# One reduction over a pair of banks for each row maximum, two score banks, and a new grouping of the exponential sums in layer 1

## What is computed

```python
h = ada_norm(x, cond)                                   # layer 0: LayerNorm, scale and shift; layer 1: LN and modulation
q, k, v = h @ wq, h @ wk, h @ wv                        # 16 heads of 32; layer 0 with rotary; layer 1 with 4 key heads
a = softmax(q @ k.T / sqrt(32))                         # over 1024 keys
x = x + (a @ v) @ wo                                    # gated in layer 1
x = x + gelu(norm(x) @ w1 + b1) @ w2 + b2               # 512 -> 2048 -> 512, gated in layer 1
```

## Time and profile before

| | |
|---|---|
| median of the runs shown | 4044.38 us (4036.17 to 4044.77, 3 runs) |
| the profiled execution: time, span | 4039.97 us, 4038.1 us |
| TensorE's mean granted clock in it | 0.975 |
| attention of sequence 6 (layer 1): its blocks 0 to 6, its last block | about 3138 to 3346 us, 3346 to 3382 us of the span |
| attention of sequence 0 (layer 0) | about 129 to 435 us |
| start, before the first attention | 0 to 129 us |

### The profile page before, as it was taken

One profiled execution on the slowest core, in us unless ns is written; L12 is line 12 of the kernel. 1 busy time (PEld: TensorE's weight loads), 2 busy tenths in 40 slices (PEclk: granted clock), 3 DMA queues, 4 the chain that ended last, 5 costly groups with the idle time before them and its releaser, 6 DMA issues.

```text
span 4038.1 us, 53506 instructions
## 1 busy us (share of the span) xinstructions
PE 3800.2 (94%) x20400; PEld 1502.4 (37%) x20400; DVE 2466.3 (61%) x3903; ACT 1603.3 (40%) x2807; POOL 1711.6 (42%) x955
## 2 busy tenths in 40 slices
PE   6988899998999989999899998999899998999999
PEld 4322344333543335433254323432244333533244
DVE  4687645765457755576555777367664776467742
ACT  1365312653125632155421653136511563136521
POOL 2376412673216742066510664037510673126620
PEclk9899999999999999999999999999999999999999
DMA  4232243212423223332233022311222112311122
GB/s 143 52 99 91 97 106 86 71 54 82 107 78 81 59 74 89 100 82 59 85 100 94 17 62 69 111 40 25 82 80 90 30 38 79 113 53 25 61 66 94
DMA packets 138973, 305.21 MB, mean 76 GB/s; under 512 B 19632, under 2 KB 59588, under 8 KB 137824
## 3 DMA queue, kind: packets, MB, share of 16 engines
q10 hardware_dynamic: 50944, 174.62, 13.4%
q1 hardware_dynamic: 87776, 127.17, 12.1%
HBM read 223.46 MB, written 36.66 MB: 64 GB/s over the span
## 4 chain that ended last, share of the span: by engine, by line
PE 80%; DVE 9%; POOL 4%; issue 3%; ACT 3%; DMA 1%; SPq 0%; ACTq 0%; POOLq 0%; DVEq 0%
PE ps L806 12%; PE ps L807 12%; PE ps L808 12%; PE ps L986 10%; PE ps L907 9%; PE ps L969 8%; PE ps L843 7%; PE ps L1001 5%; DVE mcol L1476 3%; PE ps L860 2%; POOL sums L702 2%; ACT probs L1157 2%; DVE ring L1526 2%; PE ps L824 1%; DVE dcopy L1493 1%
## 5 line engine op out<-in xcount | busy, mean ns | idle before, releaser
L702 POOL TENSOR_TENSOR sums<-probs 128x1024 f32<-128x1024 f32 x496 | 1175.6, 2384 | 1039.5 <-PE ps L1001 570.0
L1476 DVE TENSOR_REDUCE mcol<-ps 128x1 f32<-128x512 f32 x2048 | 1289.4, 682 | 454.0 <-PE ps L907 451.6
L1157 ACT ACTIVATE probs<-ps 128x512 f32<-128x512 f32 x2048 | 1098.9, 607 | 854.0 <-PE ps L969 617.6
L907 PE MATMUL ps<-ks,qs 97*128 97x512 f16 x2048 | 790.6, 388 | 64.4 <-DVE mcol L1476 47.0
L969 PE MATMUL ps<-qs,ks 98*128 98x512 f16 x2048 | 776.6, 389 | 77.4 <-ACT probs L1157 73.0
L1302 ACT ACTIVATE sums<-ps,cols 128x512 f32<-128x512 f32 x256 | 175.9, 687 | 1153.9 <-PE ps L808 1153.9
L986 PE MATMUL ps<-probs,v_sb 128*32 128x512 f32 x4096 | 568.0, 631 | 0.0
L907 PEld LDWEIGHTS ps<-ks,qs 97*128 97x128 f16 x2048 | 199.7, 98 | 624.9 <-DVE mcol L1476 375.2
L806 PE MATMUL ps<-ring,probs 128*128 128x512 f16 x1024 | 390.8, 382 | 20.6 <-DVE probs L1572 20.6
L806 PE MATMUL ps<-aT,ring 128*128 128x512 f16 x1024 | 388.3, 379 | 6.5 <-ACT dcopy L1169 6.5
L807 PE MATMUL ps<-ring,probs 128*128 128x512 f16 x1024 | 390.3, 381 | 0.0
(11 more groups left out here) (106 smaller groups left out, 3273.7 us busy)
## 6 DMA issues: line engine op xcount, KB each, us to landing
ring<-halves ACTq DMA_DIRECT2D x208, 512.0 KB, 3.4
qs<-hl SPq DMA_DIRECT2D x192, 128.0 KB, 4.0
ring<-halves SPq DMA_DIRECT2D x48, 512.0 KB, 6.4
ring<-in_weights ACTq DMA_DIRECT2D x39, 512.0 KB, 4.3
halves<-ring ACTq DMA_DIRECT2D x37, 512.0 KB, 2.9
ks<-hl SPq DMA_DIRECT2D x120, 128.0 KB, 4.4
dcopy<-inverses SPq DMA_DIRECT2D x56, 256.0 KB
probs<-in_x SPq DMA_DIRECT2D x8, 1024.0 KB, 6.9
```

The source lines that it names most:

```text
L702: pool.tensor_tensor(sums[:, m % SUM_SLOTS, :, :], prob(u - 2), prob(u), ALU.add).then_inc(sum_set[0].sem, 1)
L907: pe.matmul(bank, qs[0:K_MAX, hh, h, P * qt:P * qt + P], ks[0:K_MAX, key_set(i, hh), key_head(i, hh, h), 512 * half:512 * half + 512], sta ...
L1157: act.activation(prob(u)[:, e, :], ps[:, w % SCORE_BANKS, :], ACT.Exp).then_inc(exp_done.sem, 1)
L1476: dve.tensor_reduce(mcol[:, blk % 2, 4 * j + qt, half:half + 1], src, AX.X, ALU.max).then_inc(n_free[0], 1)
```

## The change

* A row maximum is one item of two matmuls into two neighbouring banks and one reduction over 1024 elements. The two M of an item are "halves"; the item waits for both banks before its first half, and VectorE is told after the second. `mfin` and its reduction go. 16 items per block, 2 in a step.
* Banks: S has two (0 and 1), the pairs (2, 3) and (6, 7) serve M; fills and R take single banks of these four. In the forward stage M has the one pair (6, 7).
* TensorE's step is now half, S, half, V, S, (fill), S, (fill), half, half, S, then T, then R.
* Layer 1 sums the 8 key tiles of a block in groups of 3, 3 and 2: 10 adds and 3 T per block, where there were 8 adds and 4 T. VectorE makes 17 of a sequence's 80 adds. Layer 1 has 8 `probs` buffers and 4 `sums` slots, the added ones in `wqkv` and `trig`, which layer 1 doesn't need. Layer 0 keeps 6, 3, 4 T per block and its adds.
* T of a group comes 3 steps after its last unit (2 for the first two groups of layer 0); in layer 1 that is in steps 0, 2 and 5 of a block, in layer 0 in steps 0, 2, 4 and 6 as before.
* The weight split's high half on ScalarE moves half a step, its low half on VectorE a step, its store one and a half steps later.

```diff
-SCORE_BANKS, MAX_BANKS, LATER_BANKS = 3, (3, 6, 7), (6, 7)
+SCORE_BANKS, MAX_BANKS, LATER_BANKS = 2, (2, 3, 6, 7), (6, 7)
+PAIRS = (2, 6)
...
+PROBS, SUM_SLOTS = (6, 8), (3, 4)
+GROUP_KT = (((0, 1), (2, 3), (4, 5), (6, 7)), ((0, 1, 2), (3, 4, 5), (6, 7)))
+O_AT, D_AT, HI_AT, INVERT_AT, NORM_AT, LO_AT, DEVIATION_AT = 7, 11, 15, 4, (6, 7), (3, 3), (53, 67)
...
-MAX_AT_K = (0, 2, 5, 7, 9, 11, 14, 16, 18, 20, 23, 25, 27, 29, 32)
+MAX_AT = (2, 4, 6, 8, 10, 12, 14, 16)
+MAX_AT_K = (0, 2, 4, 7, 9, 11, 14, 16)
 WO_AT = 52
...
+                    if kt_ == kts_[1]:
+                        TAKEN[l_][unit_ - 2] = len(ADDS[l_])
+                    TAKEN[l_][unit_] = len(ADDS[l_])
+                    ADDS[l_].append((unit_, len(LAST_ADDS[l_]), r_, kt_ == kts_[1]))
+            LAST_ADDS[l_].append((len(ADDS[l_]) - 2, len(ADDS[l_]) - 1))
+SUMS = tuple(len(adds_) for adds_ in ADDS)
+BLOCK_SUMS = tuple(n_ // 8 for n_ in SUMS)
+GROUPS = tuple(len(last_) for last_ in LAST_ADDS)
+def totals_step(l, group):
+    if group == GROUPS[l] - 2:
+        return STEPS + 1
+    return ADDS[l][LAST_ADDS[l][group][0]][0] // 2 + (2 if l == 0 and group < 2 else 3)
+def by_vector(l, m):
+    return m in (SUMS[0] - 3, SUMS[0] - 1) if l == 0 else m % 10 in (0, 4) or m == SUMS[1] - 1
...
-        if n in (31, 32):
-            keys += [("max", j, 1, 2 * (n - 31)), ("max", j, 1, 2 * (n - 31) + 1)]
     return keys
...
 read_, recent_ = [0, 0], list(MAX_BANKS)
 def pass_through(key, banks):
-    bank = [b for b in recent_ if b in banks][0]
-    recent_.remove(bank)
-    recent_.append(bank)
-    NARROW[key], BANK[key], USER_BEFORE[key] = len(NARROW), bank, LAST_USER.get(bank)
-    LAST_USER[bank] = key
+    if key[0] == "max":
+        _, bank = min((max(recent_.index(b), recent_.index(b + 1)), b) for b in PAIRS if b in banks)
+        used = (bank, bank + 1)
+    else:
+        bank = [b for b in recent_ if b in banks][0]
+        used = (bank,)
+    before = []
+    for b in used:
...
+        def sum_buffer(i, group, r):
...
-                    sum_set[0].sem, 1)
+                if opens:
+                    if read:
+                        pool.wait_ge(d_mul.sem, d_mul.at(i, read))
+                    elif i >= 1:
+                        pool.wait_ge(f_set.sem, f_set.at(i))
+                    pool.tensor_tensor(dst, prob(i, u - 2), prob(i, u), ALU.add).then_inc(sum_set[0].sem, 1)
...
                 if layer(i) == 0:
                     turns(i, -1)
-                for m in range(SUMS):
...
                         deviation("ln2", i, 0)
-                    if m >= 8 and m % 8 == NORM_AT:
-                        normalise(i, m // 8 - 1)
-                    if m >= 16 and m % 8 == LO_AT:
-                        finish(i, m // 8 - 2)
+                    if m >= per and m % per == NORM_AT[l]:
...
+                if half == 0:
+                    if k == 0:
+                        stacks_ready(i, blk)
+                    bank_free(key)
+                j, qt = max_tile(k)
                 h = 4 * g + j
-                pe.matmul(bank, qs[0:K_MAX, hh, h, P * qt:P * qt + P],
-                          ks[0:K_MAX, key_set(i, hh), key_head(i, hh, h), 512 * half:512 * half + 512],
-                          start=True, stop=True).then_inc(n_full, 1)
...
+                if half == 1:
+                    mm.then_inc(n_full, 1)
+            def max_halves(keys):
...
+                pe.wait_ge(*freed(("max", i, blk, 15)))
+                pe.transpose(bank[0:16, 0:P], mcol[:, blk % 2, :], ident[:, :]).then_inc(n_full, 1)
...
                 mm.then_inc(d_mul.sem, 1)
             def attention(i):
                 for s in range(STEPS + LAG // 2):
                     u = 2 * s
+                    halves, fills = max_halves(maxima_at(i, s)), FILLS[i].get(s, [])
                     if s < STEPS:
-                        maxima, fills = maxima_at(i, s), FILLS[i].get(s, [])
-                        some(maxima[0:1])
+                        some_halves(halves[0:1])
                         score(i, 4 * s)
-                        some(maxima[1:2])
+                        some_halves(halves[1:2])
+                    if LAG <= u < UNITS + LAG:
+                        values(i, u - LAG)
+                    if s < STEPS:
                         score(i, 4 * s + 1)
                         for key in fills:
                             fill(key, 0, 6 if key[0] in "kqv" else 12)
-                        some(() if fills else maxima[2:3])
                         score(i, 4 * s + 2)
                         for key in fills:
                             if key[0] in "kqv":
                                 fill(key, 6, 12)
-                        some(maxima[2:3] if fills else maxima[3:4])
+                        some_halves(halves[2:4])
                         score(i, 4 * s + 3)
-                        some(maxima[3:] if fills else maxima[4:])
-                    if LAG <= u < UNITS + LAG:
-                        values(i, u - LAG)
-                    if s == STEPS + 1:
-                        totals(i, SUMS - 4)
-                    for pair in range(SUMS // 2 - 2):
-                        if s == totals_step(i, pair):
-                            totals(i, 2 * pair)
+                        some_halves(halves[4:])
+                    for group in range(GROUPS[layer(i)] - 1):
+                        if s == totals_step(layer(i), group):
+                            totals(i, group)
                     some(rows_at(i, s))
...
                             if g == FC - 1 and t < 3:
                                 mm.then_inc(y_full.sem, 1)
-                            if t == 1:
-                                some(keys[1:2] if spread(keys) else ())
                         mm.then_inc(f2_mm.sem, 1)
-                    some(keys[2:] if spread(keys) else keys)
+                    some(keys[1:] if spread(keys) else keys)
...
                 if e == 0:
-                    if u >= PROBS:
-                        act.wait_ge(v_mul.sem, v_mul.at(i, (u - PROBS) // 2 + 1))
-                        act.wait_ge(*sum_done(sum_of(u - PROBS), i))
+                    before = u - PROBS[layer(i)]
+                    if before >= 0:
+                        act.wait_ge(v_mul.sem, v_mul.at(i, before // 2 + 1))
+                        act.wait_ge(*sum_done(TAKEN[layer(i)][before], i))
                     elif u == 4 and i >= 1:
                         act.wait_ge(f2_mm.sem, f2_mm.at(i))
...
                     for q, (st, ch) in enumerate(here):
-                        if u == 2 * st:
+                        if u == 2 * st + 1:
                             split_high(i, q)
-                        if u == 2 * st + 4:
+                        if u == 2 * st + 7:
...
             def max_item(key):
                 _, i, blk, k = key
-                j, qt, half = max_tile(k)
-                src = bank_full(key)
-                dve.tensor_reduce(mcol[:, blk % 2, 4 * j + qt, half:half + 1], src, AX.X, ALU.max).then_inc(n_free[0], 1)
+                j, qt = max_tile(k)
+                bank_full(key)
+                src = ps[:, BANK[key]:BANK[key] + 2, :].rearrange("p a d -> p (a d)")
+                at_ = 4 * j + qt
+                dve.tensor_reduce(mcol[:, blk % 2, at_:at_ + 1], src, AX.X, ALU.max).then_inc(n_free[0], 1)
...
                     blk, maxima = s // 8, maxima_at(i, s)
-                    for key in maxima[0:2]:
+                    for key in maxima[0:1]:
                         max_item(key)
                     for key in FILLS[i].get(s, ()):
                         if not by_scalar(key):
                             narrow(key)
                         if key == ("wo", i, 3):
```

More of the change, by code:

```diff
@@ L111, in spread @@
 def spread(keys):
[L113 to L117 removed]
+    return len(keys) > 0 and keys[0][0] == "max"
 def rows_at(i, s):
@@ L440, in sum_done @@
         def sum_done(m, i):
-            v = int(by_vector(m))
-            return sum_set[v].sem, sum_set[v].at(i, shares[v].index(m) + 1)
+            v = int(by_vector(layer(i), m))
+            return sum_set[v].sem, sum_set[v].at(i, shares[v][layer(i)].index(m) + 1)
+        def sum_buffer(i, group, r):
+            n, slots = 2 * group + r, SUM_SLOTS[layer(i)]
+            buffer = sums[:, n % slots, :, :] if n % slots < 3 else trig[:, 1, :].rearrange("p (a d) -> p a d", a=2)
+            return buffer, (n - slots) // 2 + 1 if n >= slots else 0
         def stack_done(key):
@@ L745, in attention @@
                     turns(i, -1)
-                for m in range(SUMS):
-                    if not by_vector(m):
+                l, per = layer(i), BLOCK_SUMS[layer(i)]
+                for m in range(SUMS[l]):
+                    if not by_vector(l, m):
                         add_probs(i, m)
@@ L810, in bank_free @@
             def bank_free(key):
-                before = USER_BEFORE[key]
-                if before is not None:
+                for before in USER_BEFORE[key]:
```

(23 more changed lines are left out.)

146 lines of the change are left out of this document (79 added, 67 removed).

## The result

The changed kernel took 4266.5 us (median of 4 runs, 4266.2 to 4269.8) against 4043.1 of the kernel before in the same comparison: a ratio of 1.0558, 95% interval 1.054 to 1.0576. The direction was forecast, the size was not: +223 us where the prediction had +61 and its range ended at 4145.

A forecast was written before the change was run, and what follows sets the result against it. The prediction took PE, busy 94% of the span, as the bound. Its terms, -27 + 44 + 65 + 25 - 38 + 8 - 22 + 0 + 6 = +61, on 4040 gave 4101 us, range 4036 to 4145.

The forecast's parts named there:

- Fewer T, -27: Layer 1's blocks: each loses one T, 32 in all at 0.85 us, -27 us.
- last blocks of layer 1, -22: Last block of each layer 1 sequence: more buffers end waits for sums, 5.5 us less in each of four, -22 us.
- Parted V and T, +44: TensorE's steps: V and T no longer adjacent cost 0.21 us each, 208 times, +44 us.
- two score banks, +65: Steps with M and no fill: scores wait for exponentials, 0.20 us in 342 and 0.04 in 171, +65 us.
- step 5: M's waits for reductions on TensorE: pairs free a whole step back remove part of them, -38 us, bounds -15 and -90.
- R, +25: R waits 1.0 us for the last reduction where no T lies between, 28 times in layer 1, 4 in layer 0: +25 us.
- DVE's added adds, 0: Layer 1: DVE gets two adds of 1.23 us in a block of 26 us, at no cost.
- the start, +8: Start, with one pair for M: 16 items run one after another at 1.91 us each, +8 us.
- plain step of 3.05 us: Layer 1: a TensorE step without T would take 3.05 us, where it took 2.85.
- B: Rival, faster: M's waits for reductions hold PE for 130 us instead of 38, time 4009 us; chance 0.13.
- C: Rival, nothing: parting V and T costs nothing and the exponential chain is partly covered, time 4042 us; chance 0.07.
- D: Rival, dearer: PE, waiting in every step, is granted less clock, 50 us more, time 4150 us; chance 0.10.

The follow-up runs named there:

- banks and order: Kernel before with two banks for S, four for M and fills, and the changed kernel's TensorE order, but one reduction per M: 4177.4 us.
- before: The kernel without the change, run again beside each group of experiments: 4039.8, 4036.6 and 4040.6 us.
- maxima's part: Changed kernel with its pairs, banks and order, but layer 1's sums made as in layer 0: 4240.5 us.
- T before R: Changed kernel with layer 1's adds on GpSimd except a sequence's last, and the first group's T one step later, in R's step: 4188.1 us.
- adds on GpSimd: Changed kernel, but GpSimd makes all of layer 1's adds except the last of a sequence: 4218.4 us.
- after: The changed kernel with the whole change, against the kernel before: 4266.5 us, ratio 1.0558.

## Why the prediction was wrong

The runs divide the change into five parts, each the difference of two kernels. Beside each stands what the prediction's own prices give for it.

| part | difference | prediction's terms | measured |
|---|---|---|---|
| two score banks, V and T parted, four banks for M, single reductions | banks and order - before | 240 x 0.21 + 65 - 38 = 77 | 141 |
| reductions over pairs, one pair in the start and forward stage, later splits | maxima's part - banks and order | 8 + 6 = 14 | 63 |
| new sums on GpSimd, a T before each R | T before R - maxima's part | -27 - 22 - 32 x 0.21 = -56 | -52 |
| no T before R in layer 1 | adds on GpSimd - T before R | 25 | 30 |
| VectorE's added adds | after - adds on GpSimd | 0 | 48 |
| sum | | 60 | 230 |

The forecast as a whole was +61, and after is 227 us above its own round's `before`; the `before` of the rounds differ by 3 to 4 us.

1. *Fewer T, -27, and last blocks of layer 1, -22.* Right in the changed kernel, -52 in the table. A last block fell by 6 us there, as forecast (5.5). In the kernel before the same sums gained only 21: a last block fell from 34 to 26 us from first to last S, but 4 us per sequence came back right behind it, and the first seven blocks of the four sequences became 7 us shorter together, where 28 T at 0.85 make 24. R's waits are part of that: without a T before it R waited 24.4 us there and 10.2 before.
2. *Parted V and T, +44, and two score banks, +65.* Both gaps are in the timelines as forecast (0.32 us from S to T, 1.07 from S to the S two after it), and M's waits for single reductions went as step 5 says, and yet the part cost 141 and not 77. What the prediction did not list is what V's move does to V itself and to R. V now asks for its bank two scores earlier, and the copy stayed where it was: 17 us by its run. R lost the V before it: its waits went from 10.2 to 31.4 us, 21 more. The other 26 us are not placed.
3. *R, +25.* Right for the T that layer 1 took away: 30 measured. The waits by V's move, just named, come on top.
4. *DVE's added adds, 0.* This step failed. "DVE gets two of 1.23 us" in a block of 26 us took the duration from adds that had happened while GpSimd made none beside them. Beside GpSimd's they take 2.9 us, and cost 48 us here and 149 in the kernel before.
5. *M's waits, -38, with the start, +8.* This step failed too. It took away waits because a pair is free "a whole step back", and named the fills without a price. Four single banks bring the gain (47.0 to 10.2 us); pairs in the same banks leave 29.8 us, and with VectorE's adds in front of the reductions it is 68.9. In time the pair costs 63 us, 17 of it at the start (8 were forecast), 21 in the forward stage, where no cost was forecast, and 25 in the attentions, in part behind fills. Four banks as two pairs are two buffers, three single banks were three, and a fill in one bank of a pair blocks both.

So three steps went wrong by a similar amount: the moved V's own wait and R's (with what is not placed, 64 us), the pair (49), VectorE's adds (48). Parts that were right, such as the plain step of 3.05 us, are right by their mechanism and not by luck.

Of the rivals, B and C are out. B: PE's 375 us of weight-load waits for reductions fell to 188.9 in the changed kernel, and the time rose. C: neither the parting nor the third bank was free. D did not happen over the whole span: the mean granted clock was 0.974 after 0.975. Its 4150 lay nearer to the result than the forecast for another reason.

What stays open: the 26 us of banks and order that are not placed; how the 21 us between the attentions come about in single waits; how the 25 us in the attentions divide between fills, splits and the other cases; and how much of the pair's and the adds' price is the clock. None of them was tried by a run of its own.

## What to carry to other kernels

Two buffers made of four banks are not four buffers: before merging instructions over banks, count the users of each bank in the order of the list, fills included. A duration is only as good as its surroundings: take VectorE's from a row where GpSimd is as busy as it will be, above all for instructions with two inputs in SBUF. And when an instruction moves forward in an in-order list, price its own waits at the new place first, and then what it covered at the old one.

## What was unexpected of the hardware

A VectorE add with both inputs in SBUF, 1.15 to 1.23 us alone, does not run beside a GpSimd add of 2.36 us: it ended 1.07 us after it, also when it had started in the middle, so it shows as up to 3.4 us. The wait shows as a longer instruction and not as idle time. Reductions from PSUM were not touched by it: 1219 ns in the mean for 1024 elements, 682 for 512.
